# Scores turned as full-array products of stacked operands, in a fused attention and expert kernel

## The reference, cut to what matters

```python
q = rope(layernorm(x) @ Wq); k = rope(c @ Wk); v = c @ Wv
scores = einsum('bhqd,bhkd->bhqk', q, k) / 4
probs = softmax(scores); ctx = probs @ v
x = x + ctx @ Wo
n = layernorm(x)
gate = scatter(softmax(top16(n @ Wq_w.T @ keys.T)))
x = x + ((n @ A_w.T) * repeat(gate, 8)) @ B_w.T * 2
```

## Time and profile before

| | |
|---|---|
| median of three runs | 170.12 us |
| profiled execution, from the first to the last instruction | 168.1 us |
| TensorE matmul (PE) | 162.7 us busy, 97% |
| TensorE weight load (PEld) | 129.9 us, 77% |
| VectorE (DVE) | 134.9 us, 80% |
| ScalarE (ACT) | 89.8 us, 53% |
| GpSimd (POOL) | 91.1 us, 54% |
| granted TensorE clock | 1.000 |
| DMA moved | 13.46 MB, mean 80 GB/s |

### The profile page before, as it was taken

The page is one execution under the profiler, slowest core; times in us unless marked ns, Lnnn a source line. Parts: engine busy times, 40 slices in busy tenths (PEclk is TensorE's granted clock), DMA queues, the critical chain, the costliest instruction groups (busy, mean ns, idle before and its releaser), DMA issues.

```text
span 168.1 us, 4082 instructions
## 1 busy us (share of the span) xinstructions
PE 162.7 (97%) x1437; PEld 129.9 (77%) x1437; DVE 134.9 (80%) x394; ACT 89.8 (53%) x212; POOL 91.1 (54%) x113
## 2 busy tenths in 40 slices
PE   7999999899999999999999999999999999999993
PEld 2657786678878787879887987879888866889883
DVE  1969886986998899799887998699884988767752
ACT  3588989899656362723538234732349154333210
POOL 5479999899799654805952099206440303512100
DMA  5999952313203010210212000100010001000013
GB/s 173 361 415 388 408 161 62 129 21 105 66 7 118 4 62 0 78 52 0 64 59 69 4 0 0 64 4 0 0 66 0 0 4 62 4 0 4 0 62 125
DMA packets 6739, 13.46 MB, mean 80 GB/s; under 512 B 832, under 2 KB 1216, under 8 KB 6464
## 3 DMA queue, kind: packets, MB, share of 16 engines
q1 hardware_dynamic: 6432, 12.95, 22.7%
q10 hardware_dynamic: 288, 0.27, 0.5%
HBM read 11.11 MB, written 2.10 MB: 79 GB/s over the span
## 4 chain that ended last, share of the span: by engine, by line
PE 52%; POOL 26%; issue 11%; DVE 5%; ACT 2%; DMA 2%; POOLq 0%; ACTq 0%; DVEq 0%
PE ps_w L1234 8%; PE ps_w L1235 7%; PE ps_w L1239 7%; PE ps_t L1247 4%; POOL am_lo L330 3%; POOL k_bd_hi L374 3%; POOL wo_lo L330 3%; PE ps_s L1320 3%; PE ps_s L1339 3%; POOL wq_lo L330 3%; POOL b_lo L330 2%; PE ps_t L1234 2%; PE ps_t L1239 2%; PE ps_t L1235 2%; POOL k_bd_lo L374 2%
## 5 line engine op out<-in xcount | busy, mean ns | idle before, releaser
L921 DVE TENSOR_REDUCE ps_s<-ps_s 128x8 f32<-128x512 f32 x32 | 21.0, 689 | 0.6 <-PE ps_s L1320 0.3
L398 POOL TENSOR_TENSOR late<-late,gate 128x512 f32<-128x512 f32 x7 | 7.6, 1084 | 24.2 <-issue 17.3
L383 POOL TENSOR_TENSOR oT_lo<-o_n,oT_hi 128x512 fp32r<-128x512 f32 x8 | 10.4, 1296 | 15.7 <-ACT oT_hi L611 15.7
L603 ACT ACTIVATE eT<-ps_s 128x512 f32<-128x512 f32 x32 | 17.0, 600 | 3.4 <-PE ps_s L1345 3.4
L1234 PE MATMUL ps_w<-am_hi,x2T_hi 128*128 128x288 f32 x48 | 14.3, 320 | 0.0
L1235 PE MATMUL ps_w<-am_lo,x2T_hi 128*128 128x288 f32 x48 | 13.1, 295 | 0.0
L1234 PE MATMUL ps_w<-b_hi,zT_hi 128*128 128x512 f32 (+1 forms) x28 | 10.7, 389 | 0.0
L1227 PE MATMUL ps_w<-wq_hi,xT_hi 128*128 128x512 f32 x26 | 10.7, 411 | 0.0
L1234 PEld LDWEIGHTS ps_w<-am_hi,x2T_hi 128*128 128x128 f32 x48 | 9.0, 187 | 2.1 <-ACT late L635 0.4
L1235 PE MATMUL ps_w<-b_lo,zT_hi 128*128 128x512 f32 (+1 forms) x28 | 10.4, 376 | 0.0
L653 ACT ACTIVATE zT_hi<-ps_t 128x512 fp32r<-128x512 f32 x7 | 4.2, 598 | 11.4 <-PE ps_t L1247 11.4
(11 more groups left out here) (256 smaller groups left out, 537.2 us busy)
## 6 DMA issues: line engine op xcount, KB each, us to landing
x_sb<-x SPq DMA_DIRECT2D x8, 256.0 KB, 6.7
cT_in<-cT SPq DMA_DIRECT2D x7, 256.0 KB, 2.8
out<-res SPq DMA_DIRECT2D x7, 256.0 KB, 2.0
wq_sb<-wq SPq DMA_DIRECT2D x4, 256.0 KB, 5.4
late<-wo SPq DMA_DIRECT2D x1, 1024.0 KB, 7.7
am_sb<-aT SPq DMA_DIRECT2D x1, 1024.0 KB, 8.8
b_sb<-bT SPq DMA_DIRECT2D x1, 1024.0 KB, 7.2
xT_raw<-xT SPq DMA_DIRECT2D x4, 256.0 KB, 2.9
```

Of the source, the lines that this page charges most:

```text
L383: pool.tensor_tensor(oT_lo[:], o_n[:].rearrange("p (b r q) -> p r b q", b=2, r=REP), oT_hi[:].bitcast(F32), ALU.subtract).then_inc(oT_lo_o ...
L603: act.activation(eT[:, c].rearrange("p b n -> p (b n)"), ps_s[:, c, :], ACT.Exp)\
L921: dve.tensor_reduce(neg_top[:, b, HALF_H * half:HALF_H * (half + 1), :], ps_s[:, 2 * (1 - b) + half, :].rearrange("p (r h k) -> p h r k", ...
```

## The change

For tiles 3 to 6 the four products of a pair are made as one. The three products of 32 rows each and the one with the maxima are sums over rows, so their operands are stacked on the 128 partitions: `k_stack` holds `k_bd_hi`, `k_bd_lo`, `k_bd_hi` and `sel`, and `q_stack` holds `qT_hi`, `qT_hi`, `qT_lo` and the turned maxima. `turned_scores` of such a tile is 8 products of 128 rows by 256 columns. SP's DMAs copy the parts within SBUF: `stack_sel` once (8 DMAs), `stack_k(t)` 12 DMAs of 32 KB and `stack_q(t)` 12 DMAs of 64 KB for each of the four tiles. ScalarE's `m_out` writes the turned maxima into the last 32 partitions of `q_stack`, once for each batch, repeated for the four pairs. The two stacks lie where `am_sb` and `b_sb` lay. `turn_m` in a late step goes from behind `up_high` into its middle.

```diff
+STACKED = (3, 4, 5, 6)
...
+            def stack_sel():
+                sp.wait_ge(am_l, DK)
+                sp.wait_ge(sel_ok, 2)
+                for s in range(2):
+                    for c in range(PAIRS):
+                        rows = slice(QUAD * c, QUAD * (c + 1))
+                        sp.dma_start(k_stack[3 * QUAD:P, s, c].bitcast(F32),
+                                     sel[rows].bitcast(F32))\
+                          .then_inc(st_sel, 16)
+
+            def stack_k(t):
+                sp.wait_ge(k_bd_ok, 2 * t + 2)
+                if t - 2 in STACKED:
+                    sp.wait_ge(sT_ps, t - 1)
+                for c in range(PAIRS):
+                    rows, at = slice(QUAD * c, QUAD * (c + 1)), 2 * (c % 2)
+                    for n, part in enumerate((k_bd_hi, k_bd_lo, k_bd_hi)):
+                        sp.dma_start(k_stack[QUAD * n:QUAD * (n + 1), t % 2, c].bitcast(F32),
+                                     part[rows, t % 2, :, at:at + 2, :].bitcast(F32).rearrange("p b h k -> p b (h k)"))\
+                          .then_inc(st_k[t], 16)
+
+            def stack_q(t):
+                sp.wait_ge(qT_lo_ok, t + 1)
+                if t - 1 in STACKED:
+                    sp.wait_ge(sT_ps, t)
+                else:
+                    sp.wait_ge(b_l, DK)
+                for c in range(PAIRS):
+                    rows = slice(QUAD * c, QUAD * (c + 1))
+                    for n, part in enumerate((qT_hi, qT_hi, qT_lo)):
+                        sp.dma_start(q_stack[QUAD * n:QUAD * (n + 1), c].bitcast(F32).rearrange("p b n -> p (b n)"),
+                                     part[rows, t % 2].bitcast(F32).rearrange("p b r q -> p (b r q)")).then_inc(st_q[t], 16)
...
             load_c(5)
+            stack_sel()
             load_x(7)
             load_xT(5)
+            stack_k(3)
+            stack_q(3)
             load_c(6)
+            stack_k(4)
             store(0)
             load_xT(6)
+            stack_q(4)
             load_c(7)
+            stack_k(5)
             store(1)
             load_xT(7)
-            for t in range(2, T - 1):
+            stack_q(5)
+            stack_k(6)
+            store(2)
+            stack_q(6)
+            for t in range(3, T - 1):
                 store(t)
...
+                if t in STACKED:
+                    if t - 1 not in STACKED:
+                        act.wait_ge(b_l, DK)
+                    for b in range(2):
+                        act.activation(q_stack[3 * QUAD:P, :, b, :],
+                                       mT_bank(t)[3 * QUAD:P, :].unsqueeze(1).broadcast_to([QUAD, PAIRS, 2 * P]),
+                                       ACT.Copy).then_inc(mT_ok, 1)
+                    return
...
+            def stacked_scores(t):
+                pe.wait_ge(st_q[t], 16 * 3 * PAIRS)
+                pe.wait_ge(st_k[t], 16 * 3 * PAIRS)
+                pe.wait_ge(st_sel, 16 * 2 * PAIRS)
+                for b in range(2):
+                    for c in range(PAIRS):
+                        if b == 0 and c in (0, PAIRS - 1):
+                            pe.wait_ge(mT_ok, mT_count(t) - (c == 0))
+                        mm = pe.matmul(ps_s[:, c, 2 * P * b:2 * P * (b + 1)], k_stack[:, t % 2, c, b, :],
+                                       q_stack[:, c, b, :], start=True, stop=True)
+                mm.then_inc(sT_ps, 1)
...
-                up_high(f)
+                up_high(f, [0, 1])
                 turn_m(n)
+                up_high(f, [2, 3])
                 up_low(f)
```

More of the change, by code:

```diff
@@ L78, in build @@
         b_hi, b_lo = sb("b_hi", [P, DK, D], F32R), sb("b_lo", [P, DK, D], F32R)
-        am_sb = sb("am_sb", [P, DK, AM])
+        with nc.sbuf_tensor("am_sb", [P, DK, AM], F32) as am_sb:
+            pass
+        k_stack = sb("k_stack", [P, 2, PAIRS, 2, 2 * BATCH], F32R)
+        sb("am_rest", [P, DK * AM - 2 * PAIRS * 2 * 2 * BATCH])
         late = sb("late", [P, REP, D])
         wo_sb, x2, z_sb, zg = late[:], late[:, 0:2, :], late[:, 2, :], late[:, 3, :]
-        b_sb = sb("b_sb", [P, DK, D])
+        with nc.sbuf_tensor("b_sb", [P, DK, D], F32) as b_sb:
+            pass
+        q_stack = sb("q_stack", [P, PAIRS, 2, REP * BATCH], F32R)
         warm = sb("warm", [P, D], mybir.dt.bfloat16)
@@ L158, in build, with mT_count @@
         ROUTE = ps_s[:, :, 0:E]
+        def mT_count(t):
+            return t + 1 + sum(1 for s in STACKED if s <= t)
         def z_bank(t, half):
@@ L250, in build @@
         up_ps, res_ok, stored = sem("up_ps"), sem("res_ok"), sem("stored")
+        st_q = {t: sem(f"st_q{t}") for t in STACKED}
+        st_k = {t: sem(f"st_k{t}") for t in STACKED}
+        st_sel = sem("st_sel")
         block = ctx.enter_context(nc.Block())
@@ L1331, in turn_m @@
                 mm.then_inc(m_ps, 1)
+            def stacked_scores(t):
[9 more added lines that the diff above has]
+                mm.then_inc(sT_ps, 1)
             def turned_scores(t):
-                pe.wait_ge(mT_ok, t + 1)
+                if t in STACKED:
+                    stacked_scores(t)
+                    return
+                pe.wait_ge(mT_ok, mT_count(t))
                 for b in range(2):
@@ L1604, in last @@
                 turn_zg(a)
-                pe.wait_ge(mT_ok, T)
+                pe.wait_ge(mT_ok, mT_count(T - 1))
                 turn_x2(l)
```

## The result

The changed kernel took 168.45 us (median of four runs: 168.98, 167.93, 167.92 and 172.5), the kernel before 169.98 (four runs, 169.71 to 170.38). The run of 172.5 was a disturbed one; it and three later ones of its kind are left out of every ratio and every pooled median in this document. The ratio is 0.990, with a 95% interval of 0.986 to 0.994. All 19 remaining runs of the changed kernel together have a median of 168.62 us, just inside the range, against 169.75 for the 40 runs of the kernel before that were measured beside the last two: 1.1 us.

What follows compares the result with a forecast made beforehand. TensorE was taken as the bound from tile 3 to 6; 0.15 at tile 3 plus 3 x (0.30 - 0.05), about 1.0 us, took 170.12 to 169.1 us. The range was 168.6 to 170.4.

Steps and rivals of the forecast that it cites:

- The bound: From tile 3 to tile 6 TensorE is wholly busy; work taken from it comes off the end one for one.
- Streaming and seams: Turned scores on TensorE: eight equal passes either way, streaming gains nothing; three seams of 0.10 vanish, 0.30 us a tile.
- the term of tiles 4 to 6: Seam gain on TensorE of 0.30 us in each of three late steps, before a charge of 0.05 each.
- `turn_m`: Moved into `up_high` at tiles 4 to 6, its wait for `m_split` loses its cover: charged 0.05 us a step.
- ScalarE: `m_out` becomes two copies of 1.02 us, 1.96 together; tile 3 ends at 69.08, gaining 0.15; later tiles have room.
- Rival B: Repeated copies in `m_out` on ScalarE cost 1.54 us each: a loss of 0.45, 170.6 us; 5 in 100.
- SP: 24 DMAs a tile, 0.46 us each, occupy 11 us of an 18.7 us step; landing takes 2.9; all hidden, no cost.
- tightest of the four: `stack_q(3)`: twelfth copy issued at 62.9, landing at 65.8, needed at 67.99, 2.2 us to spare.
- rival A: SP too slow for tile 3: wait 11p - 7.25, beginning at p = 0.66; 170.7 us at 0.80; 10 in 100.
- The sum: Gain over tiles 3 to 6: 0.15 + 3 x (0.30 - 0.05) = 0.90 us, up to 1.2, about 1.0 taken.
- The time and the range: Whole kernel: profiled 168.1 becomes 167.1, carried by 2.0 to a median of 169.1 us; range 168.6 to 170.4.

Runs made afterwards that it cites:

- e3: Kernel before with the turned scores of tiles 3 to 6 as eight whole-array products, no stacks, low parts and maxima left out: 168.57 us, ratio 0.992.
- e2: Kernel before with only `turn_m` moved into the middle of `up_high` in the late steps: 169.65 us, ratio 1.001.
- e7: Changed kernel with six DMAs of 96 partitions in place of 24 of 32 a tile, three quarters of the bytes: 168.69 us, ratio 0.993.
- e6: Changed kernel with four more DMAs of 32 KB, into unused memory, at the head of each `stack_q`: 176.52 us, ratio 1.038.
- e1: Changed kernel measured a second time, no edit: 168.99 us against 169.74 for the kernel before, ratio 0.995.
- e5: Changed kernel measured a third time, no edit, on another chip: 168.53 us, ratio 0.992 to the kernel before.
- e4: Changed kernel with stacks issuing high parts first, once ready, and `stack_k(3)` ahead of `load_x(7)` and `load_xT(5)`: 168.17 us, ratio 0.991 to the kernel before.
- e8: Changed kernel with SP's order changed (high parts first, `stack_k(3)` earlier), measured a second time on another chip: 168.26 us, ratio 0.992 to the kernel before.

## Why the prediction was right or wrong

**The bound, right.** TensorE was the limit, and what was taken from it came off the end: 75.44 against 76.25 in the steps, 167.3 against 168.1 in the span, both 0.8.

**Streaming and seams: the mechanism right, the size too small.** The products keep 0.12, so packing four tiles of 32 rows gained and lost nothing; transposes and products together take 1.40, forecast 1.38. The Trainium skill, "TensorE: Matmul & The Clock Gate", Part 3, has about 4 ns for each further tile in the span of a pack. The estimate from it, 0.10 more a tile, counted that for every pack in a row; here the next pack starts 0.118 us on and the next whole product 0.119, and the account below closes without it. But I counted three seams of 0.10 up to the start of `project_down` and took its first product for an ordinary one. It had a share too, 0.23 to 0.24 to its successor against 0.13. From `turn_q` to the second product of `project_down` after takes 1.53 (86.07 to 87.60) where before took 1.91 (1.68 and 0.23), and each late step of e3 is 0.38 shorter than before. So the price is 0.38 us a tile, not 0.30, and the term of tiles 4 to 6 should have been 1.14 instead of 0.90.

**`turn_m`, right and free.** e2 puts the charge at zero, 0.15 less than I took for the three steps; no wait stands at 83.57.

**ScalarE, right.** The lines of after, page and timeline:

```profile
L655 ACT ACTIVATE q_stack<-ps_s 32x1024 fp32r<-32x1024 f32 x8 | 7.7, 1011 | 4.2 <-PE ps_s L1392 4.2
```
```profile
66.41 1.93 ACT L655 ACTIVATE q_stack<-ps_s 32x1024 fp32r<-32x1024 f32 x2 [2.78 <-PE ps_s L1392]
```

1.01 us a copy, 1.93 for both (forecast 1.02 and 1.96), although each reads its 256 columns four times. Rival B falls. At tile 3 the eight products take longer, as said, since the fourth has to wait for the second copy, which ends at 68.34:

```profile
67.92 1.33 PE L1404 MATMUL ps_s<-q_stack,k_stack 128*128 128x256 f32 x8
69.08 0.30 PE L1297 MATMUL ps_w<-am_hi,x2T_hi 128*128 128x288 f32 x1
```

1.16 in place of 1.04, and the end at 69.08 is the forecast one. The step gives 0.17 where e3 gives 0.30. It is ScalarE and not SP: e7, with its six copies, has the same 19.86.

**SP, wrong: this step failed in the profile.** I took p, the time from one issue to the next, as 0.46 from loads of 256 KB out of HBM, with bounds of 0.37 to 0.73. A copy within SBUF costs 0.59 to 0.60 and 0.04 to the next. The timeline of SP in after:

```profile
65.23 0.59 SPq L322 DMA_DIRECT2D q_stack<-qT_lo  x1
65.87 0.58 SPq L290 DMA_DIRECT2D cT_in<-cT  x1
...
94.97 0.43 SPq L278 DMA_DIRECT2D xT_raw<-xT  x1
...
97.37 1.96 SPq L322 DMA_DIRECT2D q_stack<-qT_hi  x2
...
103.17 0.59 SPq L322 DMA_DIRECT2D q_stack<-qT_lo  x1
```

So p is 0.64, 24 of them 15.2 us of a step of 18.4, not 11. Tile 3, the "tightest of the four", held: its last copy was issued at 65.23 (forecast 62.9), and it came in time because landing takes 2.0 us and not the 2.9 of the loads. That tile 3 held is luck: the error in p, and `stack_q(3)` starting at 58.30 behind a `stack_k(3)` that took until 58.2 and not 55.5, were in part made good by the error in the landing. (The estimate of 0.47 us for a transfer was not put to the test: SP issued only every 0.64 us.) By the formula of rival A the wait at tile 3 begins at p = 0.66 with 2.9 us of landing; with 2.0 it begins at 0.74. The real slack at tile 3 was 67.92 less 67.2, or 0.7 us, not 2.2. e6 shows the far side of that edge: the last copy was issued 3.16 later (68.39), and tile 3 ended 2.40 later (71.48 against 69.08), 3.16 less the slack.

The failure is at tile 5. `stack_k(5)` begins at 85.95, and behind it stand `store(1)`, `load_xT(7)` and `stack_q(5)`, 26 issues. `load_xT(7)` was to land at 95.0 for a reader at 97.06; it was issued at 94.97 and landed near 97.8. `stack_q(5)` was to be ready with "5 us or more"; its last copy was issued at 103.17, after the two long entries named above, and landed at 105.2, while TensorE could have begun at 104.83, 0.36 behind its transposes. The PE timeline of after:

```profile
104.47 0.60 PE L1310 MATMUL ps_t<-ident,q_r 128*128 128x128 f32 x4
105.24 1.22 PE L1404 MATMUL ps_s<-q_stack,k_stack 128*128 128x256 f32 x8 [0.17 <-DMA q_stack<-qT_lo]
```

That is 0.41 us late, of which the profile calls 0.17 idle, since it models the ends of products. In e1 the same lateness of SP entered by the other door, `load_xT(7)`, ScalarE, VectorE and `k_r`. This is rival A's mechanism at another tile, at a smaller p than I gave it. Three profiles without a wait would not show by themselves that SP is the cause, since e5, with nothing changed, has none either. But e4 and e8 change only SP's order and what it waits for, and they have no wait in spite of longer entries than those of after; e7 changes the number of its DMAs (and a quarter of the bytes), and its last copy is issued nearly 14 us ahead of its use (91.33 for 105.1); the step is 18.37 to 18.39 in all three. e6 adds to the number, and the waits grow. Together with the landing times, that shows it.

**The sum, right by two errors.** Forecast 0.9 to 1.2 in the span, 1.0 taken. Measured 0.8 in the profile: 1.43 for the seams up to tile 6, less 0.13 at tile 3, less 0.45 at tile 5, less some 0.04 elsewhere. Where tile 5 is in time it is 1.27. Over all runs it is 1.1. The seams gave 0.24 more than forecast and `turn_m` 0.15; tile 5 took as much away again.

**The time and the range, wrong by the step from span to time.** I wrote that the profiled 168.1 "lies 2.0 below the median" and carried these 2.0 over to 167.1. But in every run whose span is on record, of each kernel here, the time is 1.7 to 1.9 us above its own span, mostly 1.7 or 1.8. The execution profiled was a better one than the median run, by up to 0.3, and the three runs shown were themselves high: 40 later ones have a median of 169.75. With 1.7 the same 167.1 gives 168.8, and the range would have begun at 168.3. The second part is spread. I allowed 0.3 for it, while the 19 runs of the changed kernel lie between 167.92 and 169.81. Their median, 168.62, is 0.5 below the forecast and just inside the range, so that the four runs first measured fell outside it is in part the draw. Two sources of it are seen in the profiles: tile 5, 0.45 that comes and goes, and the start. The point before any edited work of TensorE lies between 48.71 and 49.52 in the table. The two runs near 167.92, with spans of 166.2, weren't profiled; a start like e4's and no wait at tile 5 would give 166.3, but that they had these is inferred.

**The other order.** 12 runs have a median of 168.17, against 168.62 for the changed kernel and 169.75 for the one before. The 0.45 between the first two is the size of the wait at tile 5, but that wait is not in every execution, so the match is not a proof. The intervals of the ratios overlap (0.990 to 0.994 and 0.991 to 0.994 on the second chip), and e7, which has no wait either, stands at 168.69 with a late start of 49.52. The profiles show that the wait is gone, and the times are in keeping with it; more they don't prove.

## What to carry to other kernels

When small products run in packed tiles among whole-array ones, price the switches first, the first product behind them too; merging pays by the seam, not by the pass. When the means is DMAs, find their issue price on the queue that sends them, multiply by all that stands in one step, and follow the last item of the queue as closely as the first, loads for other engines included: the tightest place was not the one with the shortest deadline but the one with the longest queue ahead. Leave room for single issues that take double. And carry a forecast from the profiled span to the time by what lies around that same execution, not by the distance to the median of other runs.

## What the runs showed of the hardware

- **Issuing.** A copy within SBUF took SP 0.59 to 0.62 us at 32, 64, 96 or 192 KB (after and e7); a load or store issued right behind one mostly took 0.58 to 0.59, one further away 0.33 to 0.44. The median from issue to landing was 1.9 to 2.1 us on 32 partitions, 2.2 to 3.1 on 96. Single entries took longer (1.27; pairs of 1.96, in e6 one of 2.28), and in every profile of a changed kernel some of them stood at tile 5; why is open.
- **Switches.** One excursion of TensorE from 128-row products to four tiles of 32 rows and back, here for eight passes, cost 0.38 us over four places (after and e3 against before).
- **The clock.** In e6 TensorE stood idle twice for about 2.2 us. Behind the first (to 70.42) the granted clock stayed at 1.00; behind the second (to 91.24) it was 0.50 for 3.2 us, from about 92.8 to 96. The profile of after, with a wait of 0.4, shows 1.00 in that stretch. So a long wait can cost more than itself; what made the second differ from the first is open.
- **The start, in part open.** The whole spread in front of tile 2 has arisen by 7 us. From the first transposes of `xh` (6.20 to 7.16) to the first product behind tile 2 nine of the ten profiles take 42.34 to 42.39 us and e4 42.51. Ahead of them stand four fp32 products, and two things move them. One is when the first of them starts (5.17 to 6.20). It was latest in e7, held by the load of c, and the late 49.52 of e7 comes from that alone:

```profile
6.20 1.10 PE L1494 MATMUL ps_w<-wkv_sb,cT_in 128*128 128x256 f32 x4 [1.33 <-DMA cT_in<-cT]
```

The other is their own length, here in after first and in e4 second:

```profile
L1497 PE MATMUL ps_w<-wkv_sb,cT_in x2: 634/700/767, 5.3 to 5.8; 128*128 128x256 f32 x2
```
```profile
L1497 PE MATMUL ps_w<-wkv_sb,cT_in x4: 379/379/454, 5.2 to 5.9; 128*128 128x256 f32 x4
```

Both profiles give a granted clock of 1.00 in this stretch, and the code up to there is the same. The four products take 1.56 to 1.76 us to the transposes in before, after, e1 and e2, 1.45 in e3, and 0.93 to 1.10 in the others. Why one execution has the one and another the other was not found.
